# Attention row-sum reciprocals spread through DRAM instead of through TensorE

## The reference

```python
# x: (2, 1024, 256); w_aq: (G=4, H=4, 256, 128); w_ak, w_av: (4, 256, 128); w_ao: (4, 4, 128, 256)
q = rope(einsum('bim,ghmd->bghid', x, w_aq)); k = rope(einsum('bim,gmd->bgid', x, w_ak))
v = einsum('bim,gmd->bgid', x, w_av)
s = einsum('bghid,bgjd->bghij', q * D ** -.25, k * D ** -.25) - 1e30 * causal_mask
p = softmax(s, axis=-1)                      # exp(s - max) / sum(exp(s - max))
r = einsum('bghid,ghdm->bim', einsum('bghij,bgjd->bghid', p, v), w_ao)
x = layernorm(x + r)
x = layernorm(x + routed_experts(x) + silu(x @ ws_gate) * (x @ ws_up) @ ws_down)
```

## Time and profile before

| | |
|---|---|
| median of 3 runs | 1159.41 us (1158.77 to 1160.17) |
| the profiled execution | 1157.38 us |
| its span, first to last instruction | 1155.7 us |
| PE busy | 1036.8 us (90%) |
| DVE busy | 621.9 us (54%) |
| ACT busy | 525.0 us (45%) |
| POOL busy | 390.9 us (34%) |
| mean granted PE clock | 0.963 |

### The profile page before, as it was taken

One profiled execution on the slowest core, in us unless ns is written; L12 is line 12 of the kernel. 1 busy time (PEld: TensorE's weight loads), 2 busy tenths in 40 slices (PEclk: granted clock), 3 DMA queues, 4 the chain that ended last, 5 costly groups with the idle time before them and its releaser, 6 DMA issues.

```text
span 1155.7 us, 16797 instructions
## 1 busy us (share of the span) xinstructions
PE 1036.8 (90%) x5472; PEld 750.2 (65%) x5472; DVE 621.9 (54%) x1613; ACT 525.0 (45%) x1162; POOL 390.9 (34%) x417
## 2 busy tenths in 40 slices
PE   4689999999999999988899999999999999666725
PEld 3577777777777767666677767777777676434412
DVE  3547565445565755635575553565657656322316
ACT  2434455546454554542344555564546545132312
POOL 3212332624335233023313336243342420134641
PEclk8899999999999999998999999999999999878968
DMA  9500110000000000000000000000000082977458
GB/s 297 146 14 11 53 41 10 21 10 7 19 5 23 6 3 20 5 3 25 20 6 20 21 10 16 11 2 19 6 15 6 2 199 71 243 233 167 55 101 309
DMA packets 67316, 65.00 MB, mean 56 GB/s; under 512 B 10545, under 2 KB 61605, under 8 KB 67232
## 3 DMA queue, kind: packets, MB, share of 16 engines
q1 hardware_dynamic: 53856, 51.85, 15.7%
q0 software_dynamic: 9216, 6.76, 3.9%
q10 hardware_dynamic: 4160, 5.31, 1.4%
HBM read 40.83 MB, written 36.44 MB: 67 GB/s over the span
## 4 chain that ended last, share of the span: by engine, by line
PE 72%; DVE 8%; DMA 7%; issue 5%; POOL 4%; ACT 2%; SPq 1%; ACTq 0%; POOLq 0%
PE o_ps L921 20%; PE s_ps L897 15%; PE ring L872 11%; PE ring L910 10%; PE ring L936 8%; DMA sums<-erow,goal_u 6%; PE ring L878 3%; SPq L603 1%; PE s_ps L900 1%; PE ring L927 1%; DVE q_sin L1081 1%; POOL slot_rows L675 1%; DVE neg_max L1097 1%; POOL q_rot L663 1%; DVE q_cos L1079 1%
## 5 line engine op out<-in xcount | busy, mean ns | idle before, releaser
L921 PE MATMUL o_ps<-pt,v_sb 128*128 128x512 f32 x576 | 294.6, 594 | 2.9 <-DVE ot L1125 2.0
L768 ACT ACTIVATE pt<-ring 128x512 f32<-128x512 f32 x288 | 171.0, 594 | 267.9 <-PE ring L910 267.8
L760 ACT ACTIVATE probs<-s_ps,neg_max 128x128 f32<-128x128 f32 (+7 forms) x256 | 189.5, 741 | 152.1 <-DVE neg_max L1097 145.1
L1097 DVE TENSOR_REDUCE neg_max<-s_ps 128x1 f32<-128x128 f32 (+7 forms) x256 | 191.1, 750 | 94.8 <-PE s_ps L900 94.3
L910 PE MATMUL ring<-ident,probs 128*128 128x128 f32 x1152 | 175.5, 275 | 5.2 <-ACT probs L760 4.7
L897 PE MATMUL s_ps<-kt_hi,qt_hi 128*128 128x512 f32 (+3 forms) x384 | 165.0, 430 | 2.4 <-DVE qt_lo L1034 2.4
L910 PEld LDWEIGHTS ring<-ident,probs 128*128 128x128 f32 x1152 | 129.0, 142 | 53.3 <-issue 52.4
L663 POOL TENSOR_TENSOR q_rot<-q_cos,q_sin 128x256 f32<-128x256 f32 x80 | 63.9, 799 | 235.3 <-DVE q_sin L1081 232.1
L675 POOL DMA_INDIRECT slot_rows<-row,slot_u x96 | 97.6, 1017 | 109.4 <-DVE slot_u L1223 85.0
L897 PE MATMUL s_ps<-kt_hi,qt_lo 128*128 128x512 f32 (+3 forms) x384 | 133.1, 347 | 0.0
L897 PE MATMUL s_ps<-kt_lo,qt_hi 128*128 128x512 f32 (+3 forms) x384 | 132.8, 346 | 0.0
(11 more groups left out here) (160 smaller groups left out, 1442.9 us busy)
## 6 DMA issues: line engine op xcount, KB each, us to landing
fsum<-sums SPq DMA_DIRECT2D x32, 256.0 KB, 6.6
sums<-blank SPq DMA_DIRECT2D x16, 384.0 KB
wexp<-in_L_ffn_w_gate_dram SPq DMA_DIRECT2D x32, 192.0 KB, 6.0
wexp<-in_L_ffn_w_up_dram SPq DMA_DIRECT2D x32, 192.0 KB, 6.5
wexp<-in_L_ffn_w_down_dram SPq DMA_DIRECT2D x32, 192.0 KB, 7.9
slot_rows<-blank SPq DMA_DIRECT2D x1, 5184.0 KB, 28.5
srow<-slot_rows ACTq DMA_DIRECT2D x1, 2592.0 KB, 22.4
x_sb<-in_L_attn_x_dram SPq DMA_DIRECT2D x16, 128.0 KB, 2.0
```

Source lines behind the costliest of these rows:

```text
L760: act.activation(probs[:, u % 2, h, 0:blocks(u) * P], s_ps[:, n % 2, score_cols(n)], ACT.Exp, bias=neg_max[:, n % 8:n % 8 + 1], accum_out= ...
L768: reader(act.activation(pt[:, n % PTB, :], bank(s), ACT.Copy), s)
L921: pe.matmul(o_ps[:, :], v_sb[:, j, g * D:(g + 1) * D], pt[:, n % PTB, :], start=(j == 0), stop=(j == blocks(u) - 1)).then_inc(pv_done, 1)
L1097: dve.tensor_reduce(neg_max[:, n % 8:n % 8 + 1], s_ps[:, n % 2, score_cols(n)], AX_X, ALU.max, negate=True).then_inc(max_ready, 1)
```

## The change

All 64 units are treated alike. At a unit's first `ptrans`:

- DVE takes the reciprocal of the 128x4 row sums. It waits for the probabilities and, from the third unit on, for the store out of the same half of `inv_sum` two units ago.
- SP waits for it and stores the 128x4 reciprocals to a DRAM tensor `inverses`, head by head (each number apart: 512 pieces of 4 bytes). SP then waits for that store, and for the `omul` two units back, and loads the 512 numbers as one row into all 128 partitions of `inv_row`, which now has two buffers.
- `omul` waits for that load and multiplies `o_ps` by `inv_row`.

The steps `linv` (PE transposes, ACT copy) and `scale` (DVE) are gone, and PE's `ptrans` waits for the probabilities alone. `linv` no longer takes a bank of the `ring`. Apart from this, `SEQ` is the same. Further, ACT does one 128x1 Sigmoid after attention, ahead of its wait for the scattered rows.

```diff
-SCALED_FROM = 6
...
     def product():
         u, j = waiting.pop(0)
-        if j == blocks(u) - 1:
-            seq.extend([] if scaled_first(u) else [("linv", u)])
         seq.append(("pv", u, j))
...
-RINGED = ("xt", "proj", "qkt", "ptrans", "linv", "outproj", "x1t", "rtr", "ht", "count", "sd")
+RINGED = ("xt", "proj", "qkt", "ptrans", "outproj", "x1t", "rtr", "ht", "count", "sd")
...
+    inverses = nc.dram_tensor("inverses", (2, P * H), F32, kind="Internal").ap()
...
-        inv_row = sb("inv_row", [P, HD], F32, att)
+        inv_row = sb("inv_row", [P, 2, HD], F32, att)
...
         # SP
+                if s[0] == "ptrans" and s[2] == 0:
+                    u = s[1]
+                    sp.wait_ge(inv_ready, u + 1)
+                    sp.dma_start(inverses[u % 2, :].rearrange("(h p) -> p h", h=H), inv_sum[:, u % 2, :],
+                                 allow_slow_non_contiguous=True).then_inc(inv_stored, 16)
+                    sp.wait_ge(inv_stored, 16 * (u + 1))
+                    used(sp, o_ready, u - 1)
+                    sp.dma_start(inv_row[:, u % 2, :],
+                                 inverses[u % 2:u % 2 + 1, :].to_broadcast([P, P * H])
+                                 ).then_inc(inv_loaded[u % 2], 16)
...
         # ACT
-                if kind == "linv":
...
-                    reader(act.activation(inv_row[:, :], bank(s), ACT.Copy), s)
...
             act.wait_ge(attention_left, 1)
+            act.activation(act_cell[:, :], minus_half[:, :], ACT.Sigmoid)
             act.wait_ge(z_stored, 16 * TILES)
...
         # PE
-                    if scaled_first(u):
-                        pe.wait_ge(scaled_ready, SCALED_AT[H * u + H - 1] + 1)
-                    else:
-                        pe.wait_ge(probs_ready, H * (u + 1))
+                    pe.wait_ge(probs_ready, H * (u + 1))
...
-                if kind == "linv":
-                    u = s[1]
-                    pe.wait_ge(inv_ready, INV_AT[u] + 1)
-                    for h in range(H):
-                        ins = pe.transpose(bank(s)[:, h * P:(h + 1) * P],
-                                           inv_sum[:, u % 2, h:h + 1].to_broadcast([P, P]), ident[:, :])
-                    ins.then_inc(linv_ready, 1)
...
         # DVE
-                if kind == "scale":
-                    u, h = divmod(s[1], H)
-                    dve.wait_ge(probs_ready, s[1] + 1)
...
-                    after(dve.reciprocal(inv_sum[:, u % 2, h:h + 1], row_sum[:, u % 2, h:h + 1]))
-                    dve.tensor_scalar(p, p, inv_sum[:, u % 2, h:h + 1], None, ALU.mult).then_inc(scaled_ready, 1)
-                if kind == "ptrans" and s[2] == 0 and not scaled_first(s[1]):
+                if kind == "ptrans" and s[2] == 0:
                     u = s[1]
                     dve.wait_ge(probs_ready, H * (u + 1))
...
+                    used(dve, inv_stored, 16 * (u - 1))
                     dve.reciprocal(inv_sum[:, u % 2, :], row_sum[:, u % 2, :]).then_inc(inv_ready, 1)
                 if kind == "omul":
...
-                        read(dve, ("linv", u))
+                    dve.wait_ge(inv_loaded[u % 2], 16 * (u // 2 + 1))
                     dve.wait_ge(pv_done, PT_AT[(u, blocks(u) - 1)] + 1)
...
-                    if scaled_first(u):
-                        dve.tensor_copy(ot[:, g, :], o_ps[:, :]).then_inc(o_ready, 1)
-                    else:
-                        dve.tensor_tensor(ot[:, g, :], o_ps[:, :], inv_row[:, :], ALU.mult).then_inc(o_ready, 1)
+                    dve.tensor_tensor(ot[:, g, :], o_ps[:, :], inv_row[:, u % 2, :], ALU.mult).then_inc(o_ready, 1)
```

More of the change, by code:

```diff
@@ L61 @@
 BLOCKS_IN_TURN = [n for names in SPLIT_AT.values() for n in names]
-def scaled_first(u):
-    return blocks(u) >= SCALED_FROM
 def blocks(u):
@@ L225 @@
 PT_ALL = len(PT_AT)
-SCALED_AT = {s[1]: n for n, s in enumerate(s for s in SEQ if s[0] == "scale")}
-INV_AT = {s[1]: n for n, s in enumerate(s for s in SEQ if s[0] == "linv")}
 PROJ_AT = {s[1:]: n for n, s in enumerate(s for s in SEQ if s[0] == "proj")}
@@ L388, in build @@
         inv_ready = sem("inv_ready")
-        scaled_ready = sem("scaled_ready")
-        linv_ready = sem("linv_ready")
+        inv_stored = sem("inv_stored")
+        inv_loaded = [sem(f"inv_loaded{n}") for n in range(2)]
         o_ready = sem("o_ready")
@@ L768, in _ @@
                     reader(act.activation(pt[:, n % PTB, :], bank(s), ACT.Copy), s)
-                if kind == "linv":
-                    u = s[1]
-                    act.wait_ge(linv_ready, INV_AT[u] + 1)
-                    if u >= 1:
-                        act.wait_ge(o_ready, u)
-                    reader(act.activation(inv_row[:, :], bank(s), ACT.Copy), s)
                 if kind == "x1t":
```

18 lines of the change are left out of this document (2 added, 16 removed).

## The result

The changed kernel takes 1194.26 us, the median of 4 runs (1193.51 to 1195.03), against 1159.09 (1158.54 to 1160.17) for the kernel before on the same chip: a ratio of 1.0299, with a 95% interval of 1.0283 to 1.0316. It is 35 us slower where 16 us faster was forecast. The profiled execution took 1195.03 us.

A forecast was written before the change was run, and what follows sets the result against it. PE, busy 90%, was taken as the bound. 1157.4 - 14.1 - 2.0 + 0.5 = 1141.8 us profiled, 1143.8 as a median, stated as 1143.5; forecast 1139 to 1148 us (0.60), 8 in 10 from 1136 to 1153.

The forecast's parts named there:

- I take the quiet rows with a bit for the many pieces: Round trip through DRAM on SP: 0.4 + 2.5 for the store, 0.4 + 3.3 for the load, 6.6 us in all.
- my mechanism from it, 5.0 us: Store of 4-byte pieces: 0.05 us a piece, doubled for reading and writing, store 5.0 us, round trip 9.1 us.
- the high end of 15.1: Upper bound of the DRAM round trip: 0.4 + 7.7 + 0.4 + 6.6 = 15.1 us.
- The slower rival: Slow small writes make the round trip the bound and `omul` late in many units: 1177 us at 15 us; chance 0.10.
- The weights: End of attention: second weight batch starts 7.4 us later, charged 0.5 us; with a 7.7 us store, some 3 us over.
- `z_sb` land at 1018.5 us: End of attention: `z_sb` lands behind the shifted weights at about 1018.5 us; slots loaded at 1019.64, after the last scatter.
- the idle stretch swallows a small shift: After attention, DMA engines nearly idle until 1019.6 us absorb the weights' 7.4 us shift.
- The gain on PE: Attention: removing the reciprocals' transposes saves 14.1 us, fewer PE waits for `omul` 2.0 us.
- PE's busy time: Sign to look for: PE's busy time down by about 24 us, the sum of L927 in its own measure.
- DVE's scalings give nothing: Attention: DVE loses 96 scalings, 76.3 us, but has idle time around them, so by themselves they give nothing.
- the early table is worth nothing: ACT's early sigmoid moves a 1.28 us table load; worth 0 to 1.28 us, taken as 0.
- `omul` as a product costs nothing: DVE, after a unit's last product: `omul` as a product instead of a copy takes 0.69 us either way.

The follow-up runs named there:

- experiment 5: Changed kernel with its 4-byte pieces stored query by query, 8 B apart; load waits but reads constants, division left out: 1147.15 us.
- experiment 9: Changed kernel with its 4-byte pieces stored head by head, 64 B apart; load waits but reads constants, division left out: 1142.17 us.
- experiment 1: Changed kernel with the store query by query in 128 pieces of 16 B, `omul` reading `inv_row` at a stride of 4: 1147.02 us.
- Experiment 4: Kernel before, with the second batch of expert weights held until the third product of the last unit: 1164.04 us.
- 2: Changed kernel with its 4-byte store, but the load reads constants without waiting for the store; division left out: 1173.69 us.
- 7: Kernel before, with only the 24 units of 6 blocks and more moved to the DRAM path, 4-byte store included: 1168.86 us.
- experiment 6: experiment 1 without the early Sigmoid on ACT, so the table load falls into the first pair of experts again: 1149.36 us.

## Why the prediction was wrong, step by step

**The step that failed: "I take the quiet rows with a bit for the many pieces", the store at 2.5 us and the load at 3.3.** The choice was by rows of `z_sb` and `cos_sb`, whose pieces are large. From the issue of the store to the issue of its load, where the prediction has 0.4 + 2.5 = 2.9 us, the 64 stores took:

| store | pieces | median us | shortest to longest |
|---|---|---|---|
| after | 512 of 4 B, adjacent, head by head | 9.71 | 7.50 to 13.95 |
| experiment 5 | 512 of 4 B, 8 B apart, query by query | 4.02 | 3.09 to 7.55 |
| experiment 9 | 512 of 4 B, 64 B apart, head by head | 2.00 | 1.76 to 3.69 |
| experiment 1 | 128 of 16 B, adjacent, query by query | 1.41 | 1.39 to 5.52 |

So neither number nor size of the pieces makes 8 us and more. In a run of 64 B of DRAM stand 16 pieces in the first row, 8 in the second, 1 in the third and 4 in the last, and in the first row all 16 come from different partitions. The time goes up where many pieces share a short run of DRAM. Why that is slow, no run shows; none varied the distance between 8 and 64 B either, so the size of the run isn't measured.

The rule I weighed (the Trainium skill, page "DMA: Bandwidth & Descriptors", section "Specifications": at least 512 B a piece, read-modify-write below) pointed the right way, and my mechanism from it, 5.0 us, was nearer than the 2.5 I took. But experiments 9 and 1 have pieces far under 512 B too and take 2.00 and 1.41 us, so it isn't the size alone.

The load was mis-sized too: from issue to use 5.1 us at unit 3 and 5.62 at unit 63, against 3.3; in the 17 units whose `omul` waited for it, 3.20 to 6.56 us, median 5.26. The trace of before had a nearer row than those chosen, the load of `bias_sb`, which also spreads one row to all 128 partitions: 5.2 us, in the opening burst. At unit 63 the whole is 15.42 us at a free SP, above the high end of 15.1.

**The price of a late row.** The slower rival, 1177 us at 15 us, had the right place and mechanism and was still 17 us short. It compared each unit's cover with a fixed round trip. But store, wait and load are serial on SP, and two units' cannot overlap: behind unit 2, unit 3 was late before its store was issued, by 5.3 us. Tiles 0 and 1 of both batches cost 22.7 + 13.7 = 36.4 us, where the rival's own shortfalls for these tiles (units 3, 6, 7, 35, 38 and 39, at 15 us) add up to 19.8.

**The weights.** The store decides here too. They started 5.3 us ahead of the last `omul` instead of 18.2, so 12.9 us later in place of 7.4, and the loss was 7.8 us: the prediction had "some 3 us over" for such a store. What it had wrong is the order at the end. It let `z_sb` land at 1018.5 us, ahead of the last scatter. In the changed kernel POOL issues that scatter at 1046.45 us, 24.5 us after the last `omul` (before 25.2), but `z_sb` is issued only at 1050.83, behind weights that still fill the DMA engines, and lands 7.00 us later. The slots wait for it.

How much of this is the late start is only in part shown. Experiment 4 starts the weights as late and loses 3.5 us in its trace. The three kernels with store and load of the slow kind at the last units (after, 2 and 7) take 169.6 to 171.2 us from the last `omul` to the end, all others 162.6 to 167.1, before 163.4. SP took 33.4 us to issue the batch in the changed kernel and 27.3 in experiment 4; why, stays open. Nor is it shown that the idle stretch swallows a small shift. Experiment 9 starts the weights 11.8 us ahead of the last `omul` and takes 163.5 us from there on, no more than before; but experiments 1 and 6, at 12.8 us ahead, take 165.8.

**What held.** The gain on PE: 14.1 + 2.0 us forecast, and in experiment 9 the last `omul` is at 976.22, 16.1 us earlier (in experiment 5, 15.5). That the sum fits to the tenth is partly luck: PE's waits for `omul` did not go, they are 4.5 us there instead of 2.0, and of the tiles with 1 or 2 blocks, priced at 3.5 us, the four give 7.0 (2.0 in the first batch, 4.9 in the second), those with 3 to 5 blocks 8.5 instead of 10.6. PE's busy time falls by 18.8 us there, not by 24: the sum of L927 in its own measure (0.60 us for four) overlaps its neighbour, and 40 x 0.44 = 17.6 was the one to expect. That DVE's scalings give nothing held (experiment 7; and in experiment 9 the tiles with 6 to 8 blocks gain 0.5 and 0.2 us). That the early table is worth nothing held (experiment 6). That `omul` as a product costs nothing held (690 ns), unless it is strided (1071).

**The sum, closed.** The spans: after 1193.2, experiment 9 1139.7. Of the 53.5 us between, 1021.96 - 976.22 = 45.7 are in attention, and 7.8 behind the weights. Of the 45.7, PE idles for 35.0 us more, and for 10.8 us more it is busy with the same instructions (935.1 against 924.3 us up to the last `omul`), at a granted clock of 0.97 instead of 0.99. So by these rows the late reciprocals cost PE twice: the wait, and the lower clock that goes with it. What the change itself does on the engines is about the forecast; the store's layout, with the queue behind it, is the difference.

## What to carry to other kernels

An operation that no row of the profile shows needs a bound for its own access pattern: ask not only how many bytes and pieces it has, but how many pieces from different partitions fall into the same short run of DRAM. If many do, write whole partition rows and let the reader undo the order, even at a price: here it paid, 1147 us against 1194. For a load look for a row with the same pattern, however small. A wait that stands on a queue's engine is paid in series: compare the round trip with the interval between units as well as with each unit's cover, and ask what else is queued behind it.
